# Attention by four heads and 512 queries: four 32-wide value tiles, softmax sums on GpSimd, and W_down kept in DRAM

## The reference, cut to what matters

```python
result = embeddings @ w_qkv                      # split into q, k, v of 16 heads x 32
scores = jnp.einsum('bnqd,bnkd->bnqk', q, k) / jnp.sqrt(jnp.float32(h))
ctx = jnp.einsum('bnqk,bnkd->bnqd', jax.nn.softmax(scores, axis=-1), v)
x = _layernorm(x + ctx)
h = jax.nn.silu(fp4_linear(x, w_gate)) * fp4_linear(x, w_up)
x = _layernorm(x + fp4_linear(h, w_down))
```

## Time and profile before

| | |
|---|---|
| time, median of 3 runs (range) | 4508.9 us (4506.7 to 4509.33) |
| profiled execution: span, first to last instruction | 4507.4 us; its own device time is not listed apart |
| busy: TensorE, VectorE, ScalarE, GpSimd | 93%, 71%, 41%, 14% |
| transfers | 126.76 MB, mean 28 GB/s |
| granted TensorE clock, mean | 0.980 of full speed |

### The profile page before, as it was taken

One profiled execution on the slowest core, in us unless ns is written; L12 is line 12 of the kernel. 1 busy time (PEld: TensorE's weight loads), 2 busy tenths in 40 slices (PEclk: granted clock), 3 DMA queues, 4 the chain that ended last, 5 costly groups with the idle time before them and its releaser, 6 DMA issues. The chain is left out here.

```text
span 4507.4 us, 59394 instructions
## 1 busy us (share of the span) xinstructions
PE 4203.1 (93%) x23081; PEld 1721.7 (38%) x23081; DVE 3206.1 (71%) x5179; ACT 1857.5 (41%) x2168; POOL 610.8 (14%) x670
## 2 busy tenths in 40 slices
PE   3499999999999999999999999999999999999999
PEld 2233344333533344333443334433353334433344
DVE  9856687667866678666876668766786667856688
ACT  3245433453334533445334543345333453344533
POOL 4300022001210012100220002200121001210022
PEclk8599999999999999999999999999999999999999
DMA  4110001010010100011001000101001010001100
GB/s 157 32 34 27 17 22 37 15 29 22 21 30 17 41 13 19 28 28 29 17 24 32 27 17 22 37 15 29 22 22 30 17 41 13 19 27 29 29 17 22
DMA packets 80509, 126.76 MB, mean 28 GB/s; under 512 B 21056, under 2 KB 23104, under 8 KB 80192
## 3 DMA queue, kind: packets, MB, share of 16 engines
q1 hardware_dynamic: 80192, 122.51, 9.4%
HBM read 53.22 MB, written 16.78 MB: 16 GB/s over the span
## 5 line engine op out<-in xcount | busy, mean ns | idle before, releaser
L492 DVE TENSOR_REDUCE mx<-R 128x1 f32<-128x512 f32 x2080 | 1386.7, 690 | 911.3 <-PE R L576 909.0
L1020 ACT ACTIVATE arena<-SC 128x1024 f32<-128x1024 f32 x1024 | 996.7, 1022 | 968.2 <-PE SC L1302 967.9
L1397 PE MATMUL SC<-wgu,split 128*128 128x512 f16 (+1 forms) x4608 | 935.5, 361 | 6.8 <-ACT split L1059 3.6
L1397 PEld LDWEIGHTS SC<-wgu,split 128*128 128x128 f16 x4608 | 445.9, 98 | 469.5 <-DVE arena L1192 10.2
L1320 PE MATMUL CT<-arena,v_even 128*33 128x512 f32 x2048 | 531.1, 606 | 9.1 <-ACT arena L1013 9.1
L1320 PE MATMUL CT<-arena 128*33 128x512 f32 x2048 | 523.5, 603 | 0.0
L1412 PE MATMUL CT<-wd,arena 128*128 128x512 bf16 x2112 | 476.7, 379 | 0.0
L946 POOL TENSOR_TENSOR x<-x,ctx_new 128x256 f32<-128x256 f32 x128 | 105.3, 823 | 2401.8 <-DVE ctx_new L1124 2401.8
L556 PE MATMUL R<-xT,wqkv 128*128 128x512 bf16 x1632 | 411.2, 385 | 1.5 <-ACT xT L454 1.3
L576 PE MATMUL R<-ks_even,qs_even 96*128 96x512 bf16 x1056 | 399.6, 400 | 8.0 <-DVE mx L492 2.9
L576 PE MATMUL R<-arena 96*128 96x512 bf16 x1024 | 379.1, 384 | 5.5
(11 more groups left out here) (111 smaller groups left out, 3749.9 us busy)
## 6 DMA issues: line engine op xcount, KB each, us to landing
x<-n_L_attn_embeddings_dram SPq DMA_DIRECT2D x136, 256.0 KB, 2.9
arena<-split SPq DMA_DIRECT2D x384, 64.0 KB, 2.0
out_dram<-x SPq DMA_DIRECT2D x64, 256.0 KB, 2.0
qs_even<-split SPq DMA_DIRECT2D x204, 64.0 KB, 2.0
ks_even<-split SPq DMA_DIRECT2D x204, 64.0 KB, 2.0
x<-in_L_ffn_w_up_dram SPq DMA_DIRECT2D x13, 256.0 KB, 2.8
x<-in_L_attn_w_qkv_dram SPq DMA_DIRECT2D x4, 768.0 KB, 6.6
x<-in_L_ffn_w_gate_dram SPq DMA_DIRECT2D x11, 256.0 KB, 4.5
```

Source lines behind the costliest of these rows:

```text
L492: nc.vector.reduce_max(mx[:, j:j + 1], ring_of(ring, n)[:, :], AX_X).then_inc(max_done, 1)
L1020: nc.scalar.activation(probs[:, s % 2, hd, :], SC[hd][:, :], ACT.Exp, scale=SCALE).then_inc(exp_done, 1)
L1397: last = nc.tensor.matmul(GU[kk % 2][which][:, 0:w], xhT[:, part_x * KH + k, :], wgu[:, part_w * KH + k, which * I + first:which * I + fir ...
```

## The change

Attention is cut into units of 4 heads (a group) by 512 queries, 8 units of 8 steps. A step has the same four score matmuls and the same two exps; SC0 and SC1 now hold two heads each. The values lose their column of ones, and a step's four fp32 value matmuls of 32 columns go into the four 32-row column tiles of one bank of CT, behind each other in one block. The row sums are made apart: `acc` adds up the probabilities over the key tiles, on GpSimd for tiles 1 to 6 (two instructions of 128x1024 a step; the first reads tiles 0 and 1) and on VectorE for tile 7 (128x2048); a "sum" job multiplies `acc` by a tile of ones, ScalarE copies the result, "sumT" transposes it, and VectorE takes reciprocals. There are three buffers of probabilities. One of them, `acc`, `ctxT` and the copied sums lie in the SBUF of `wd`, so W_down is written to DRAM once, at the end of the first block, and read back in each batch behind the last "ctx" job, in six transfers. Each unit has one "ctx" job and one context add on GpSimd, 128x512. The neg transpose stands in the fourth place of step 7. The high part of the negated maxima is made by a second reduction. The columns of ones and the clearing of CT go.

```diff
-PAIRS = HEADS // 2
+UNITS = 2 * GROUPS
+UNIT_TILES = TILES // 2
+BUFS = 3
+POOL_SUMS = TILES - 2
...
-LAST_CTX = 5
-def pair_jobs(p, t):
-    ends = p == PAIRS - 1
+SUM_STEP, SUM_T_STEP, CTX_STEP = 1, 3, 4
...
+def unit_jobs(u, t):
+    ends = u == UNITS - 1
     counts = MAX_STEPS_LAST if ends else MAX_STEPS
-    m = [("max", p + 1, n) for n in range(sum(counts[:t]), sum(counts[:t + 1]))]
-    if p % 2 == 0 and (QK_JOBS if p == 0 else 0) <= t < (PROJ_JOBS if p // 2 + 1 < GROUPS else PROJ_JOBS - 1):
-        proj = [(kind, p // 2 + 1, t) for kind in ("proj_a", "proj_b", "proj_c")]
-        return m[0:1], proj[0:1] + m[1:2] + proj[1:2] + m[2:3] + proj[2:3], m[3:4], m[4:]
+    m = [("max", u + 1, n) for n in range(sum(counts[:t]), sum(counts[:t + 1]))]
     other = []
-    if p > 0 and t == (2 if ends else TILES - 2):
-        other += [("ctx", p - 1, 0)]
-    if p > 0 and t == (3 if ends else TILES - 1):
-        other += [("ctx", p - 1, 1)]
-    if ends and t == LAST_CTX:
-        other += [("ctx", p, 0)]
-    if p == PAIRS - 3:
+    if u > 0:
+        other += [("sum", u - 1, 0)] if t == SUM_STEP else []
+        other += [("sumT", u - 1, 0)] if t == SUM_T_STEP else []
+        other += [("ctx", u - 1, 0)] if t == CTX_STEP else []
+    if u % 2 == 0 and (QK_JOBS if u == 0 else 0) <= t < (PROJ_JOBS if u // 2 + 1 < GROUPS else PROJ_JOBS - 1):
+        proj = [(kind, u // 2 + 1, t) for kind in ("proj_a", "proj_b", "proj_c")]
+        return m[0:1], proj[0:1] + m[1:2] + proj[1:2] + m[2:3] + proj[2:3], m[3:4], m[4:] + other
+    if u == UNITS - 3:
         other += [("xT", t, 0)]
     if t == TILES - 1 and not ends:
-        other = [("neg", p + 1, 0)] + other
-    if p == PAIRS - 3:
-        return m[0:1], m[1:2], m[2:3] + other, m[3:]
-    if other:
-        return m[0:1], m[1:2] + other, m[2:3], m[3:]
-    return m[0:1], m[1:2], m[2:4], m[4:]
+        other = [("neg", u + 1, 0)] + other
+    return m[0:1], m[1:2], m[2:3], m[3:4] + other + m[4:]
...
-        m = [("max", PAIRS, n) for n in range(sum(MAX_STEPS_LAST), MAX_JOBS)]
-        return m, [], [("xhT", 1, 0)], [("ctx", PAIRS - 1, 1), ("neg", PAIRS, 0)]
+        m = [("max", UNITS, n) for n in range(sum(MAX_STEPS_LAST), MAX_JOBS)]
+        return (m + [("sum", UNITS - 1, 0)], [("sumT", UNITS - 1, 0)], [("xhT", 1, 0)],
+                [("ctx", UNITS - 1, 0), ("neg", UNITS, 0)])
...
-        v_odd, at = carve(at, TILES * GROUP * (HD + 1), F32)
-        pr_f, at = carve(at, 2 * 2 * S, F32)
-        ctxT, at = carve(at, S, F32)
+        v_odd, at = carve(at, TILES * GROUP * HD, F32)
+        pr_f, at = carve(at, (BUFS - 1) * GROUP * BANK, F32)
         assert at <= WORDS
-        qs = [qs_even, qs_odd.rearrange("p (h n) -> p h n", h=GROUP)]
+        qs = [qs_even, qs_odd.rearrange("p (a h n) -> p a h n", a=HALVES, h=GROUP)]
         ks = [ks_even, ks_odd.rearrange("p (h n) -> p h n", h=GROUP)]
         v = [v_even, v_odd.rearrange("p (t h d) -> p t h d", t=TILES, h=GROUP)]
-        probs = pr_f.rearrange("p (b h n) -> p b h n", b=2, h=2)
+        wd_f = wd[:, :, :].rearrange("p k n -> p (k n)").bitcast(F32)
+        WIDE = GROUP * BANK
+        p_wd, acc_f, ctxT, sumT = (wd_f[:, a:b] for a, b in (
+            (0, WIDE), (WIDE, 2 * WIDE), (2 * WIDE, 2 * WIDE + BANK), (2 * WIDE + BANK, 2 * WIDE + 2 * BANK)))
+        probs_f = [p_wd] + [pr_f[:, n * WIDE:(n + 1) * WIDE] for n in range(BUFS - 1)]
+        probs = [f.rearrange("p (h n) -> p h n", h=GROUP) for f in probs_f]
+        acc = acc_f.rearrange("p (h n) -> p h n", h=GROUP)
...
+        wd_kept = nc.dram_tensor("wd_kept", [P, 2 * KI, H], BF16, kind="Internal").ap()
...
-                    link(nc.vector.tensor_copy(neg2[:, HI, :], neg[:, :]))
+                    link(nc.vector.tensor_reduce(neg2[:, HI, :], mx[:, :].rearrange("p (m k) -> p m k", k=HALVES),
+                                                 AX_X, ALU.max, negate=True))
...
+                elif kind == "sum":
+                    pe.wait_ge(last_sum, a + 1)
+                    for hd in range(GROUP):
+                        last = nc.tensor.matmul(ring_of(ring, n)[HD * hd:HD * (hd + 1), :], ones[:, :], acc[:, hd, :],
+                                                start=True, stop=True)
+                elif kind == "sumT" or kind == "ctx":
+                    src = ctxT
+                    if kind == "ctx":
+                        pe.wait_ge(ctxT_done, a + 1)
+                    else:
+                        src = sumT
+                        pe.wait_ge(sumT_done, a + 1)
+                    for i in range(UNIT_TILES):
+                        last = nc.tensor.transpose(ring_of(ring, n)[:, i * P:(i + 1) * P], src[:, i * P:(i + 1) * P],
+                                                   identf[:, :])
...
+                sp.wait_ge(wT_done, 2 * DOWN_ROUNDS)
+                sp.dma_start(wd_kept, wd[:, :, :]).then_inc(wd_saved, 16)
+                sp.wait_ge(wd_saved, 16)
...
+                    def load_down(c):
+                        if c == 0:
+                            sp.wait_ge(pv_done, len(steps))
+                            sp.wait_ge(ring_full, ring.full(("ctx", UNITS - 1, 0)))
+                        k, n = TILE_K * c, chunk_tiles(c)
+                        for part in range(2):
+                            sp.dma_start(wd[:, part * KI + k:part * KI + k + n, :],
+                                         wd_kept[:, part * KI + k:part * KI + k + n, :]).then_inc(wd_loaded[c], 16)
...
+                    for c in range(len(CHUNKS)):
+                        load_down(c)
...
+                    def add(u):
+                        pool.wait_ge(ctx_done, u + 1)
+                        rows, g = slice(u % 2 * UNIT_TILES, (u % 2 + 1) * UNIT_TILES), u // 2
+                        xa = x[:, rows, g * P:(g + 1) * P]
+                        nc.gpsimd.tensor_tensor(xa, xa, ctx_new[:, :, :], ALU.add).then_inc(added, 1)
+                    def sum_probs(u, t, i):
+                        s, hs = TILES * u + t, slice(2 * i, 2 * i + 2)
+                        pool.wait_ge(exp_done, 2 * s + i + 1)
+                        if t == 1:
+                            if u >= 1:
+                                pool.wait_ge(ring_full, ring.full(("sum", u - 1, 0)))
+                            first = probs_of(s - 1)
+                        else:
+                            pool.wait_ge(pool_sum, sums_done(u, t - 1, i))
+                            first = acc
+                        nc.gpsimd.tensor_tensor(acc[:, hs, :], first[:, hs, :], probs_of(s)[:, hs, :],
+                                                ALU.add).then_inc(pool_sum, 1)
+                    for u in range(UNITS):
+                        for t in range(1, TILES - 1):
+                            for i in range(2):
+                                sum_probs(u, t, i)
+                            if t == CTX_STEP and u >= 1:
+                                add(u - 1)
...
+                    def context(u):
+                        act.wait_ge(pv_done, TILES * (u + 1))
+                        if u >= 1:
+                            act.wait_ge(ring_full, ring.full(("ctx", u - 1, 0)))
+                        nc.scalar.activation(ctxT, CT[:, u % 2 * BANK:(u % 2 + 1) * BANK], ACT.Copy).then_inc(ctxT_done, 1)
+                    def sums(u):
+                        n = ring.number[("sum", u, 0)]
+                        act.wait_ge(ring_full, n + 1)
+                        if u >= 1:
+                            act.wait_ge(ring_full, ring.full(("sumT", u - 1, 0)))
+                        nc.scalar.activation(sumT, ring_of(ring, n)[:, :], ACT.Copy).then_inc(sumT_done, 1)
+                    def probs_free(s, i):
+                        if i == 0:
+                            act.wait_ge(pv_done, s + 1)
+                        u, t = divmod(s, TILES)
+                        if t == TILES - 1:
+                            act.wait_ge(last_sum, u + 1)
+                        else:
+                            act.wait_ge(pool_sum, sums_done(u, max(t, 1), i))
+                    for s, (u, t) in enumerate(steps):
+                        for i in range(2):
+                            act.wait_ge(scores_done, 2 * s + i + 1)
+                            if s >= BUFS:
+                                probs_free(s - BUFS, i)
+                            nc.scalar.activation(probs_of(s)[:, 2 * i:2 * i + 2, :].rearrange("p h n -> p (h n)"),
+                                                 SC[i][:, :], ACT.Exp, scale=SCALE).then_inc(exp_done, 1)
...
+                            act.wait_ge(pool_sum, sums_done(UNITS - 1, POOL_SUMS, 1))
                         silu(i, 0)
+                        if i == 0:
+                            sums(UNITS - 1)
...
+                    def last_sums(u):
+                        s = TILES * (u + 1) - 1
+                        dve.wait_ge(exp_done, 2 * s + 2)
+                        dve.wait_ge(pool_sum, sums_done(u, POOL_SUMS, 1))
```

(44 more changed lines are left out.)

254 lines of the change are left out of this document (102 added, 152 removed).

## The result

The changed kernel takes 4914.3 us (median of 4 runs, 4903.0 to 4931.9) for 4508.9: a ratio of 1.090, 95% interval 1.088 to 1.093. Forecast were 4605 us and 4350 to 4760. The sign was right, the size was not. The profiled execution spans 4901.3 us, at a mean granted clock of 0.915 for 0.980.

The account below looks back on a forecast made before the run. TensorE was taken to set the pace. Unit terms summed to +10.3 us a batch, eight times 82; with the save +96 on 4508.9, about 4605 us. Range 4350 to 4760 us.

Parts of the forecast that it names:

- (a): Value matmuls: four 32-wide tiles overlap in one block's time, 0.99 us, saving 8.6 us of TensorE in each unit.
- rival 3: Value tiles go as two pairs, 0.86 us more in 64 steps, giving some 5000 us; chance 0.06.
- (b): Ring of maxima: VectorE's latency with two banks holds a plain step at 3.8 us, where TensorE's own work is 3.0.
- rival 1: The ring keeps up, plain steps under 3.3 us, 4363 us; chance 0.35, including what lies between it and no change.
- (c): Softmax sums on GpSimd: 12 adds at 2.12 us plus a 1.3 us context add, 26.7 us in a unit.
- rival 2: GpSimd is the bound, deciding above 2.6 us an add; at 2.9 us an add, 4840 us; chance 0.11.
- (d): VectorE's last sum takes 2.3 us and delays step 1's maxima; steps 0 and 1 of a projection unit take 14.0 us.
- (e): Two more ring jobs: the sums' transposes in step 3 and the context's in step 4, 0.65 us each.
- (f): Unit boundary: the unit ends at 5.1 us of step 7, plus 1.0 us (nothing to 2.1) for the subtraction beside GpSimd.
- (h): Into the FFN: GpSimd's adds delay its start to 46.7 us from 37.7; with idle-clock loss, unit 7 gains 11.2 us.
- (g): Sums by unit: 34.2 us without projection, 47.3 with; unit 0 at 33.4; unit 5 at 43, +4 from port meetings.
- (i): W_down: its reload in each batch is hidden, at 11.6 us; its one-time save costs 14 us.

Follow-up runs that it names:

- kernel 10: kernel 4 (all softmax sums left out) with three PSUM banks instead of two for the ring of maxima: 4080.2 us, ratio 0.905.
- 8: kernel 6 with GpSimd's adds of each step in unit 5 waiting for VectorE's low half of x two tiles on: 4518.0 us, ratio 1.002.
- kernel 4: The changed kernel with all softmax sums left out and the context multiplied by 1: 4312.3 us, ratio 0.956.
- kernel 1: The changed kernel with the negated maxima in a PSUM ring bank, so the subtraction reads one SBUF input: 4694.0 us, ratio 1.040.
- kernel 6: kernel 1 without VectorE's last sum: TensorE's ones-matmul adds the last tile, and in unit 7 GpSimd adds steps 1 to 4 only: 4553.6 us, ratio 1.009.
- kernel 5: The changed kernel with GpSimd's two step 6 adds, in all units but the last, waiting for VectorE's negated maxima: 4782.7 us, ratio 1.061.
- kernel 2: kernel 1 with VectorE's subtraction for the low part of x replaced by a one-input reduction, leaving that part out: 4643.7 us, ratio 1.030.

## Why the forecast was wrong

- *(a) Values*: right. Four tiles take one block's time, 1.00 us. The Trainium skill, "TensorE: Matmul & The Clock Gate", Part 3, gives 2.38x for three column tiles; rival 3's estimate from it would be a block of 1.24 us. The trace does not bear that estimate out for these four fp32 tiles of 32 columns.
- *(b) The ring*: right in size (3.80 us) and in cause: a third bank takes it to 3.15 (kernel 10) and 219, 232 and 225 us off three different kernels (8, 4 and the changed one). Rival 1's step of under 3.3 us exists, but only with that bank.
- *(c) Adds*: 2.36 us for 2.12. The estimate of 2.25 us, half of the figure that the Trainium skill, "GPSIMD Engine Reference", section 3.1, gives for N=2048, was nearer than my row, whose inputs are not both fp32. It decides only where GpSimd's end is on the path, ahead of the FFN: 12 x 0.24 = 2.9 us, and the stretch is 3.4 over the forecast in batch 2 and 3.0 in the mean of the eight, 24 us in all. The point of rival 2, 2.6 us, was not reached.
- *(d) The last sum*: 2.28 us, as forecast. In unit 2 of kernel 1 steps 0 and 1 take 14.2 us for the 14.0 of the walk. But in unit 6 they take 15.8: TensorE idles 2.0 us for VectorE, and its granted clock then falls, which the walk did not have. Its timeline and windows there (kernel 1, no wait on the port near):

```profile
1042.94 2.28 DVE L1198 TENSOR_TENSOR wd<-wd,arena 128x2048 f32<-128x2048 f32 x1
...
1045.88 0.39 PE L591 MATMUL R<-arena 96*128 96x512 bf16 x1 [1.98 <-DVE mx L501]
```

```profile
1043.00:1046.00 3.00, 0.94 (x4) 0.33 (x5) 2.82 (x3) 1.62 (x2) 0.00 (x0) 1.00 0.00 0
1046.00:1049.00 3.00, 3.00 (x9) 1.03 (x8) 0.69 (x1) 0.00 (x0) 0.00 (x0) 0.54 0.00 0
```

  In kernel 1 these two steps of units 2, 4 and 6 take 14.2 us in the 6 of 24 cases with a granted clock of 1.00, 15.6 to 15.8 in the 15 with 0.89, and 17.5 in the 3 with 0.81: 34 us over 14.2 in all. Without VectorE's add (kernel 6) they take 12.9 us in all 24, at 1.00; with unit 7's last sums moved too, 140 us went.
- *(e) The two ring jobs*: right, 4.39 us for 4.45 in steps 3 and 4 of a plain unit.
- *(f) The unit's boundary*: **the step that failed.** It priced the subtraction's wait on GpSimd's port at 1.0 us (0 to 2.1) from one meeting of the two engines. There GpSimd ran one operation and then paused; at the end of a unit in attention up to four of its adds lie back to back. In the changed kernel 13 of the 64 subtractions lasted 7.0 to 7.8 us, 24 about 1.55, and 11 about 0.85. In unit 1 of batch 2 that is 7.8 us where 1.0 was put. The waits themselves sum to 138 us, 2.2 a subtraction, just over (f)'s upper bound of 2.1; the other 82 of the 220 below are the rest of what the edit gave back, the clock's losses among it. The wait also empties TensorE, and unit 2 then starts at the lower clock level, 1.2 GHz: its step 0 takes 7.2 us for kernel 1's 4.7. Part (f) had nothing for the clock, although part (h) counted it for an idle of some 10 us. The runs price the whole, clock included, at 220 us (kernel 1), and 132 of them come back if only the queue is cut (kernel 5).
- *(g) Unit 5*: the same wait, about 1 us for each of eight subtractions forecast; they cost 50 us over the kernel (kernel 2), up to 2.7 us each. In unit 1 of batches 3, 5 and 6, where the subtraction took 0.87 us, the sum held: 34.2 us, to the tenth. That is partly luck: step 0 takes 3.0 us for 1.8, step 1 6.1 for 6.7, and the last step 5.6 for 6.1. The sum of a projection unit, 47.3, left out (f)'s 1.0 us, though the subtraction stands there too (1.55 us in units 2 and 4); and 48.7 less 47.3 is 1.4 for unit 4, not 1.5.
- *(h)*: the chain of 10.8 us takes 11.06, right to 0.3 us; see (c).
- *(i)*: the reload is hidden. The gate's stretch is 176 us in kernel 4, which reloads, for 175.2 before. The save costs about 7 us, as the first unit starts at 234.9 us for 227.8, and not 14.

In sum 309 us were missing. The two waits on the port cost 270 (220 and 50). The forecast's sums, as printed, had 48 for them: 1.0 us in each of units 1 and 3 and the 4 of unit 5 (if all of it is the port's), in each of eight batches. That leaves 222. Without these terms the forecast would have been 4557 us, and kernel 2 takes 4644: another 87, of which (c) explains 24. A further 24 are the clock in steps 0 and 1 of units 2, 4 and 6, which in kernel 2 take 14.2 us at 1.00 (10 cases) and 15.6 to 17.5 at 0.81 to 0.89 (14). The other 39 are spread over stretches that the forecast took as unchanged or had too short: in kernel 1 unit 0 takes 35 to 38 us for 33.4, unit 6 46 to 49 for 44.8, and the gate's stretch 179 for 177.4 (175.2 before, and 2.2 put for the clock; 176 without sums). How much of these the clock owns, no run isolates.

The upper bound of the range held the same wrong assumption as the term: at most one of GpSimd's operations in front. It was read from the rows of the kernel before instead of from the queue that the change builds, and more of those rows would not have helped. In that kernel 112 VectorE operations ran over 0.3 us longer than the shortest of their form beside GpSimd. None of them waited past the end of the GpSimd operation it met, and in 24 cases the next one started right behind it, as here:

```profile
150.38 1.93 POOL L714 TENSOR_TENSOR arena<-arena,sc_h 128x1024 f32<-128x1024 bf16 x1 [5.10 <-DVE arena L418]
...
151.03 1.33 DVE L408 TENSOR_SCALAR inv<-inv 128x64 f32<-128x64 f32 x1
152.27 2.12 POOL L721 TENSOR_TENSOR arena<-arena 128x1024 f16<-128x1024 f32 x1
```

Line 408, elsewhere 0.19 us, ends at 152.36, at the boundary between the two. The longest of the 112, an add 768 wide of 3.89 us, met one GpSimd operation of 3.1 us; the rest is its own time.

## What to carry to other kernels

Before a stream of two-input operations goes to GpSimd, list VectorE's operations with two SBUF inputs that fall beside it. Price each at up to GpSimd's whole queue, not at one instruction, plus the clock that an idle TensorE loses; a 16-column operation can be the dearest in the kernel. Cure it at the operand (one input in PSUM, or a reduction), and only then at the queue. When a change frees a PSUM bank, ask which pair of engines waits for a bank: the one that this change kept as a second buffer for the context was worth 219 to 232 us in the ring, more than the 197 that the value tiles brought.
